# Two attention layers: stacks of queries and keys moved in rows of 2 KB, score units by heads of the keys, and the end of the first stage in another order

## The reference

```python
def layer0(x, y):                       # per batch: 128 channels x 1024
    q, k = conv(Wq0, bq0, y), conv(Wk0, bk0, y)         # 8 heads of 16 channels
    attn = softmax(q_heads @ k_heads.T / sqrt(128))
    o = conv(Wo0, bo0, attn @ conv(Wv0, bv0, x)) + x
    return (o - mean(o)) * rsqrt(var(o) + eps) * gn_w + gn_b
def layer1(h, y):                       # h, y: 32 x 128 x 1024
    q = (h @ Wq + 2 * (h @ Aq @ Bq)).heads(32)
    k = (y @ Wk + 2 * (y @ Ak @ Bk)).heads(8)           # each repeated for 4 heads of q
    v = (y @ Wv + 2 * (y @ Av @ Bv)).heads(8)
    ctx = softmax(q @ k.T / sqrt(32)) @ v
    return h + ctx @ Wo + 2 * (ctx @ Ao @ Bo)
```

## Time and profile before

| | |
|---|---|
| median of 3 runs | 1451.95 us (1450.32 to 1458.22) |
| the profiled execution: its own time | 1455.78 us |
| its span from first to last instruction | 1453.7 us |
| mean granted clock of TensorE | 0.975 |
| TensorE (PE) busy | 1361.1 us, 94% |
| VectorE, ScalarE, GpSimd busy | 917.0, 823.9, 194.5 us |
| moved by DMA | 342.34 MB in 374,128 packets, mean 235 GB/s |

### The profile page before, as it was taken

One profiled execution on the slowest core, in us unless ns is written; L12 is line 12 of the kernel. 1 busy time (PEld: TensorE's weight loads), 2 busy tenths in 40 slices (PEclk: granted clock), 3 DMA queues, 4 the chain that ended last, 5 costly groups with the idle time before them and its releaser, 6 DMA issues.

```text
span 1453.7 us, 23720 instructions
## 1 busy us (share of the span) xinstructions
PE 1361.1 (94%) x7135; PEld 1063.2 (73%) x7135; DVE 917.0 (63%) x2061; ACT 823.9 (57%) x2913; POOL 194.5 (13%) x157
## 2 busy tenths in 40 slices
PE   7999999999979999999999988879999999999998
PEld 5778887777768788888888876556666667666666
DVE  5666666656644577777776743446677757666665
ACT  4566666555631177777775735446666667666441
POOL 5433333555522000000000000000000000000000
PEclk8999999999989999999999999889999999999999
DMA  6465665887946889999998899999899999998982
GB/s 181 164 218 197 196 202 191 268 262 242 301 160 215 241 238 259 265 251 261 259 260 237 238 317 304 292 274 247 217 250 249 244 239 241 243 235 217 241 224 80
DMA packets 374128, 342.34 MB, mean 235 GB/s; under 512 B 24242, under 2 KB 304404, under 8 KB 373108
## 3 DMA queue, kind: packets, MB, share of 16 engines
q1 hardware_dynamic: 374004, 340.84, 85.2%
HBM read 224.37 MB, written 116.39 MB: 234 GB/s over the span
## 4 chain that ended last, share of the span: by engine, by line
PE 71%; DMA 13%; DVE 4%; ACT 4%; issue 3%; SPq 3%; POOL 2%; ACTq 0%; DVEq 0%; POOLq 0%
PE bank L640 21%; PE bank L677 15%; PE bank L536 10%; DMA q_stack<-lse_dram 9%; PE bank L695 6%; PE bank L724 4%; PE bank L735 4%; PE bank L486 2%; PE bank L611 2%; PE bank L596 1%; ACT lora_aT_kv L874 1%; PE bank L523 1%; SPq L1683 1%; DMA x_in<-in_x 1%; POOL o_split L1479 1%
## 5 line engine op out<-in xcount | busy, mean ns | idle before, releaser
L932 ACT ACTIVATE bank<-bank,negs 128x128 f32<-128x128 f32 x1024 | 349.1, 343 | 221.9 <-DVE negs L1188 221.6
L640 PE MATMUL bank<-hT,wq 128*128 128x512 f32 x1488 | 391.5, 403 | 0.0
L677 PE MATMUL bank<-wo,op 128*128 128x512 f32 x1344 | 353.6, 401 | 2.0 <-DVE h_blk L1265 2.0
L640 PEld LDWEIGHTS bank<-hT,wq 128*128 128x128 f32 x1488 | 267.1, 190 | 47.4
L1183 DVE TENSOR_REDUCE maxes<-bank 128x4 f32<-128x512 f32 x256 | 176.3, 689 | 189.9 <-PE bank L695 187.4
L677 PEld LDWEIGHTS bank<-wo,op 128*128 128x128 f32 x1344 | 251.2, 192 | 53.6 <-DVE op L1235 2.4
L949 ACT ACTIVATE probT<-bank 128x512 f32<-128x512 f32 x256 | 151.4, 604 | 149.8 <-PE bank L724 147.0
L932 ACT ACTIVATION_READ_ACCUMULATOR bank<-bank,negs 128x1 f32 x1024 | 211.8, 207 | 0.0
L536 PE MATMUL bank<-wkv_hi,yT 128*128 128x512 f32 x512 | 206.2, 424 | 0.0
L695 PEld LDWEIGHTS bank<-k_stack,q_stack 96*128 96x128 f32 x1024 | 152.2, 192 | 25.1 <-DMA q_stack<-q_dram 6.9
L695 PE MATMUL bank<-k_stack,q_stack 96*128 96x128 f32 x1024 | 147.3, 267 | 6.7 <-DMA q_stack<-q_dram 5.6
(11 more groups left out here) (167 smaller groups left out, 1668.3 us busy)
## 6 DMA issues: line engine op xcount, KB each, us to landing
q_dram<-q_part SPq DMA_DIRECT2D x192, 256.0 KB, 3.6
q_stack<-q_dram SPq DMA_DIRECT2D x256, 192.0 KB, 5.1
q_stack<-q_dram SPq DMA_DIRECT2D x64, 768.0 KB
k_stack<-k_dram SPq DMA_DIRECT2D x128, 192.0 KB, 4.6
y_in<-in_ctx SPq DMA_DIRECT2D x32, 512.0 KB, 4.4
x_in<-in_x SPq DMA_DIRECT2D x32, 512.0 KB, 5.2
h_dram<-h_out SPq DMA_DIRECT2D x32, 512.0 KB, 2.8
h_in<-h_dram SPq DMA_DIRECT2D x32, 512.0 KB, 6.1
```

The lines of the kernel that those rows point to most:

```text
L640: m = pe.matmul(bank(u % 2).rearrange("p (a n) -> p a n", a=2), wq[:, block, part, c, :], hT[(group + 1) % 2][:, :, of, c, :], start=c == ...
L677: mm = pe.matmul(out_bank(pair, m), op[m][:, of, c, :], wo[m][:, w, c, :], start=c == 0 and of == 0 and w == 0, stop=c == GROUP - 1 and of ...
L932: act.activation(part, part, ACT.Exp, bias=negs[:, n % RING, g:g + 1], scale=SCORE1, accum_out=sums[:, score_column(k), g, member:member + ...
```

## The change

- A unit of scores is now one head of keys with its four heads of queries, instead of one head of queries out of each of the four heads of keys. Its load is 96 rows of 2 KB that lie together in `q_dram`, instead of 96 rows of four pieces of 512 B. The matmuls are as many and as large as before. Units run through the first halves of four batches and then through the second halves (`score_half`).
- `k_dram` holds the keys as they are stacked, (3 x 32) x 4 x 128. A load of keys is 96 rows of 2 KB instead of 96 x 4 pieces of 512 B, both for the units and for the scores made again. The store of a batch's keys is six transfers of 128 pieces of 512 B, instead of two (256 pieces of 512 B and 256 of 1 KB).
- `q_part` holds two blocks of queries; three stores for two blocks, in pieces of 1 KB instead of 512 B.
- A raw piece of Wo is loaded in one transfer instead of four; mixed pieces are made one batch ahead, and the order of the pieces and their loads changes with it.
- Units start at slot 24 instead of 40, are taken in every slot up to 232, in every third up to 256, and then in five slots of 16 instead of eight. The second group of logarithms is taken at slot 224, in the middle stage.
- At the end of the first stage h of the third batch is loaded earlier, the turned h are rounded and split earlier, TensorE transposes before it projects, and the first projections wait for fewer of them.

```diff
-        k_dram = scratch("k_dram", (HALVES, P, 3, P))
+        k_dram = scratch("k_dram", (HALVES, 3 * HD, GQ, P))
...
-        for i in range(4 * GROUP + 1):
+        for i in range(4 * GROUP + 2):
             c, member = divmod(i, 4)
-            made = {0: [(0, c, 0, 0)], 1: [(3, c, 4, 4 * c + 1)], 2: [(5, c, 2, 0), (4, c, 1, 4 * c + 2)],
-                    3: [(1, c, 3, 0), (2, c, 4, 4 * c + 3)]}[member]
+            made = {0: [(2, c - 1, 4, 4 * c - 1), (0, c, 0, 0)], 1: [(6, c - 1, 4, 4 * c)],
+                    2: [(3, c, 4, 4 * c + 1), (5, c, 2, 0)], 3: [(4, c, 1, 4 * c + 2), (1, c, 3, 0)]}[member]
...
-        FIRST_SCORES, LAST_TURN = 40, QUERY_SLOTS - 4 * NC
+        FIRST_SCORES, LAST_TURN, LAST_EARLY = 24, QUERY_SLOTS - 4 * NC, QUERY_SLOTS - AHEAD - 5
...
-                if chunk == 0:
+                if w < QUERY_SLOTS:
                     log_slot[chunk] = w
-                    rest = w + 8
+                    rest = w + (4 if chunk else 8)
...
-            if w < LAST_TURN:
-                take = w % 16 != 15 and (n % GROUP or w < LAST_TURN - 5)
+            if w < LAST_EARLY:
+                take = True
             elif w < QUERY_SLOTS:
-                take = w % 2 == 0
+                take = w % 3 == 0
             else:
-                take = i in range(9 if pair in log_steps else 1, STEP, 2)
+                take = i % 3 == 1 and (i > 9 or pair not in log_steps)
...
+        def score_half(n):
+
+            group, of = divmod(n // GQ, GB * NQ)
+            q, b = divmod(of, GB)
+            return NQ * (GB * group + b) + q
...
-        FIRST_STACK_LAST = LAST_TURN - 8
+        FIRST_STACK_LAST = LAST_EARLY - 4
...
-                if quarter == 0:
-                    pe.wait_ge(S["hT_lo"], 4 * (both + 1))
+                if quarter < 2:
+                    pe.wait_ge(S["hT_lo"], 4 * both + 3 + quarter)
...
-                for g in range(GQ):
-                    m = pe.matmul(score_bank(n)[:, g * P:(g + 1) * P], q_stack[place // GROUP][SCORE_ROWS, g, member, :],
+                for j in range(GROUP):
+                    m = pe.matmul(score_bank(n)[:, j * P:(j + 1) * P], q_stack[place // GQ][SCORE_ROWS, g, j, :],
                                   k_stack[SCORE_ROWS, k % 2, g, :], start=True, stop=True)
...
-                    for g in range(GQ):
-                        sp.dma_start(w_raw[i][g * HD:(g + 1) * HD, :], rows[g, :, of]).then_inc(S[f"w_raw{i}"], DMA)
+                    sp.dma_start(w_raw[i][:], rows[:, :, of]).then_inc(S[f"w_raw{i}"], DMA)
...
-                keys = k_dram[NQ * b:NQ * (b + 1)].rearrange("q p a t -> p q a t")
-                sp.dma_start(keys[:, :, 0, :], f32(kT_sb[b % 2][:, :, 0, :])).then_inc(S[f"kv_out{b % 2}"], DMA)
-                sp.dma_start(keys[:, :, 1:3, :].rearrange("p q a t -> p q (a t)"),
-                             f32(kT_sb[b % 2][:]).rearrange("p q a t -> p q (a t)")).then_inc(S[f"kv_out{b % 2}"], DMA)
+                for q in range(NQ):
+                    rows = k_dram[NQ * b + q].rearrange("(d a) g t -> a g d t", a=3)
+                    for row, part in ((0, 0), (1, 0), (2, 1)):
+                        sp.dma_start(rows[row], f32(kT_sb[b % 2][:, q, part, :])).then_inc(S[f"kv_out{b % 2}"], DMA)
...
-                sp.dma_start(f32(q_stack[score_place[n] // GROUP][SCORE_ROWS, :, member, :]),
-                             q_dram[k, :, :, member * P:(member + 1) * P].rearrange("(g d) a n -> (d a) g n", g=GQ)).then_inc(
+                sp.dma_start(f32(q_stack[score_place[n] // GQ][SCORE_ROWS, g, :, :]).rearrange("r j n -> r (j n)"),
+                             q_dram[k, g * HD:(g + 1) * HD].rearrange("d a n -> (d a) n")).then_inc(
...
-                sp.dma_start(f32(k_stack[SCORE_ROWS, 2 + k % 2, :, :]),
-                             k_dram[k].rearrange("(g d) a t -> (d a) g t", g=GQ)).then_inc(S[f"again_in{k % 2}"], DMA)
+                sp.dma_start(f32(k_stack[SCORE_ROWS, 2 + k % 2, :, :]), k_dram[k]).then_inc(S[f"again_in{k % 2}"], DMA)
```

More of the change, by code:

```diff
@@ L190, in xattn_two_layers @@
         at[0] = q_place
+        s2_sb = sb("s2_sb", [P, BANK])
+        h_blk = [sb(f"h_blk{i}", [P, BANK]) for i in range(2)]
+        lse_rows = sb("lse_rows", [P, 1, 2, P])
+        at[0] = q_place + 4 * 2 * GB * 2 * P
         op[6] = sb("op6", [P, 2, GROUP, P], F32R)
@@ L248, in raw_in @@
                 return DMA * ((n - FIRST_Q) // 2 + 1)
-            return (DMA * NC if raw_of(n) < 2 else 0) + DMA * GQ * ((n - FIRST_O) // 4 + 1)
+            return (DMA * NC if raw_of(n) < 2 else 0) + DMA * ((n - FIRST_O) // 4 + 1)
         def raw_piece(n):
@@ L995, in scalar_program @@
                 softmax0(b)
+                if last:
+                    round_hT(0)
                 if b:
@@ L1223, in split_op @@
                 elif m == 1:
-                    dve.wait_ge(S["lse_out0"], DMA)
+                    dve.wait_ge(S["lse_out1"], DMA)
                 elif m == 6:
-                    for i in range(2):
-                        dve.wait_ge(S[f"q_out{i}"], 3 * DMA * NC * NG // 2)
+                    dve.wait_ge(S["q_out1"], 3 * DMA * NC * NG // 4)
                 elif m:
@@ L1245, in combine @@
                     if pair == 0:
-                        for i in range(2):
-                            dve.wait_ge(S[f"h_out{i}"], DMA * B // 2)
+                        dve.wait_ge(S["q_out0"], 3 * DMA * NC * NG // 4)
                     else:
@@ L1635, in put_q @@
                 for row, part in ((0, 0), (1, 1), (2, 0)):
-                    sp.dma_start(halves[:, row, :, :], f32(q_part[u % 2][:, part, :]).rearrange(
-                        "p (b n) -> p b n", b=GB)).then_inc(S[f"q_out{u % 2}"], DMA)
+                    sp.dma_start(halves[:, row, :, :], f32(q_part[pair % 2][:, part, :, :, :]).rearrange(
+                        "p b j n -> p b (j n)")).then_inc(S[f"q_out{pair % 2}"], DMA)
             def wait_queries(k):
                 last = queries_out(k)
-                for u in (last - 1, last):
-                    sp.wait_ge(S[f"q_out{u % 2}"], 3 * DMA * (u // 2 + 1))
@@ L1777, in sync_program @@
                     finish_unit(n)
-            for b in range(2, GB):
-                load_h(b)
+            load_h(3)
             write_kv(B - 1)
```

208 lines of the change are left out of this document (107 added, 101 removed).

## The result

The changed kernel takes 1495.99 us (median of 4 runs, 1491.85 to 1498.87), the kernel before 1452.95 in the runs beside it. That is a ratio of 1.029, 95% interval 1.025 to 1.033. It is 43 us slower, where the forecast was 6 us faster. The profiled execution has a span of 1495.2 us. From its page: the busy times of the engines, the granted clock and the DMA share in 40 slices of 37.4 us, and the packets.

A forecast was written before the change was run, and what follows sets the result against it. TensorE was taken as the bound in each part, leaving only its waiting to gain. Terms -27 + 0 + 2 - 9 + 28 = -6 us took 1452 to 1446 us; range 1418 to 1474, the forecast's own 1434 to 1458.

The forecast's parts named there:

- Keys and Wo on four engines, +28: First stage while Wo is prepared: transfers with outer count 4 run on four engines, making x late; +28 us, bounds 0 to +55.
- The sign to look for: While Wo is prepared: x_hi late in two batches of four, with waits for x_in and batches of 14 to 16 us.
- Larger rows, -27: Middle and last parts: 2 KB rows land stacks sooner, cutting TensorE's waits and the half clock behind them; -27 us, bounds 0 to -47.
- The small waits: TensorE's waits after 1010 us, thirteen of 0.95 us on average and one of 2.8 us: 11 us taken off.
- the wait near 870 us: TensorE's wait of 4.3 us for queries of a score unit should go, through the new order of loads.
- the long waits: Four waits from 880 to 1010 us, 21.9 us, behind 2 MB Wo loads: 1.3 us off each, 6 us with what adds up.
- Units moved, 0: 28 score units, 11.2 us, move from the last part to the middle, both bound by TensorE: sum 0.
- Late there, +2: Scores start at slot 24, six slots after their queries may be loaded; being late there adds 2 us, 0 to 6.
- The first stage's end, -9: Loading h of the third batch earlier and waiting for half of the turned h saves 9 us, 0 to -13.
- The signs: Middle part some 8 us longer than 478 us; last part 30 to 35 us shorter than 527.
- The first, free narrow transfers: Key and Wo transfers cost nothing, spread over all engines or hidden by slack: 1418 us, chance 0.22.
- The second and third: Second: narrow transfers cost more in batches 17 to 29, 1470 us, chance 0.24. Third: 2 KB rows don't help, 1464 us, 0.14.

The follow-up runs named there:

- both wide: Changed kernel, key stores and Wo loads given an outermost DRAM count of 128 instead of 4, keys and Wo rows permuted: 1454.75 us, ratio 1.001 to 1.005 to before.
- experiment 2: Kernel with both wide, stacks laid out in SBUF so each 2 KB row arrives as four pieces of 512 B: 1459.95 us, 1.005 to 1.010 to before.
- keys by column: Changed kernel, Wk and Wv columns ordered by column then head, a batch's keys in three stores, raw Wo pieces in four loads: 1461.11 us.
- Experiment 5: On the twelve-store kernel, 2 MB loads spread: 1482.81 against 1485.33 us. On keys by column, no units in slots 233 to 255: 1453.09; then seventh load later: 1451.88 us.
- experiment 4: Changed kernel with twelve key stores and four Wo loads, third batch's h load moved behind its batch's stores: 1488.60 us against 1485.33.
- experiment 1: Changed kernel, outer DRAM count 128 instead of 4: both 1454.75 us, keys alone 1468.36, Wo alone 1472.09. Kernel before, keys in six stores of count 4: 1486.08.

## Why the prediction was wrong, step by step

By its own terms, for the profiled executions: forecast -6, measured +41.5 (1495.2 against 1453.7). Two terms make up nearly all of the 47.5 us between: the relief of 27 us that did not come, and the charge of 28 us that was 20 too small.

- **Keys and Wo on four engines, +28.** Right in mechanism, and the engine count was right; the size was off. The last 14 batches took 48 us more than before: 39.5 by the narrow transfers (222.8 against 183.2 with both wide), and 8.3 that stay with both wide. The time per batch was nearly right: 61.4 us for four batches is 15.35 each, measured 15.9. I charged 12 batches instead of 14 (5 us) and took off 4 us for slack. The 0.55 us in each of 14 batches that are left (8 us) I put down to SyncE standing at its issues and to the clock (0.88 from 250 to 430 us, with both wide 0.96); no run tells the two apart. The rest, some 2 us, is that batches of before took 12.5 on average (174.9 / 14) and not 12.65. The sign to look for was wrong as well: it shows as the wait of the copy for the store of the keys, 29.5 us, and only 7.1 us for x. I had checked when x would land, and not when the buffer of the keys would be free. Before Wo is prepared a batch stayed at 11.75 us, as worked out.
- **Larger rows, -27.** This step failed. With both transfers wide, middle and last stage together are 0.1 us longer than before (+22.8 - 22.7); the rows themselves are worth some 4 us (experiment 2). It had three parts. The small waits went, though not by larger rows, and in their place TensorE waits for exponentials of ScalarE (two of its groups in the last stage, the last column its idle time: the kernel before, 926:1453, then the kernel with both wide, 947:1452).

```profile
L724 PE MATMUL bank<-q_stack,k_stack 98*128 98x512 f32 x238 | 103.6, 437 | 31.2 <-DMA q_stack<-lse_dram 29.7 <-ACT probT L949 1.1
L735 PE MATMUL bank<-probT,v_in 128*32 128x512 f32 x480 | 66.7, 628 | 0.6 <-DVE lse_rows L1211 0.4
```
```profile
L731 PE MATMUL bank<-q_stack,k_stack 98*128 98x512 f32 x238 | 101.0, 426 | 19.4 <-DMA q_stack<-lse_dram 18.8 <-ACT probT L958 0.6
L742 PE MATMUL bank<-probT,v_in 128*32 128x512 f32 x480 | 65.7, 619 | 12.9 <-ACT probT L958 12.8
```

  29.7 us of waits for lse_dram become 18.8, and 12.8 us before the contexts are new. It may be that fewer units stand between a product of scores and its context, five in 16 slots instead of eight; this is not shown, and six instead of five did not shorten the wait (13.2 us from 880 to 1445 us, against 12.2 with five, both with keys by column). The second part, the wait near 870 us, went, but the next load of keys then stood behind two loads of 2 MB, and TensorE waited 9.4 us for it. The piece of SyncE's order that I cited ended at those two loads; its next row was this load. Third, the long waits did not get 6 us shorter: from 880 to 1050 us TensorE waited 24.7 us for DMA before, and waits 34.3 us with the rows of 2 KB. Experiment 5 speaks for engines that are full there, at a share near 1, and against the order of the queue.
- **Units moved, 0.** Half right: 28 units add 11.2 us to the middle, which has 15.8 us more of busy TensorE. The remaining 4.6 us go with a granted clock of 0.98 instead of 0.99, and idle time grew from 15.7 to 22.8 us. "Late there, +2" did not occur: TensorE has no wait for queries of a unit from slot 24 on.
- **The first stage's end, -9.** Right: from the last x_hi to the projections it is 44.2 us before and 35.9 with both wide, -8.3 (39.2 in the changed kernel, -5.0). But in the kernel with both wide the last 14 batches take 8.3 us more than before, 5.1 of them in the last one (17.2 us instead of 12.1), so the stage comes out even. The number of stores of keys is not it (three of them: 184.1 us against 183.2), nor, by experiment 4, the load of h. In that last batch ScalarE stands until a piece of Wo is stored, which the kernel before does not do there:

```profile
399.53 0.62 ACT L856 CAST o_split<-w_mix 128x512 fp32r<-128x512 f32 x1 [5.07 <-DMA wo_dram<-o_split]
```

  That points at the new order of the pieces, which no run changed alone: the cause stays open.
- **The signs.** A last part 30 to 35 us shorter: 23.8. A middle 8 us longer: 23.4. The sum had made the two nearly cancel in my favour, and they do cancel.
- **The rivals.** The first, free narrow transfers, is refuted by experiment 1. The second and third both happened, 1470 and 1464 us each; I gave them apart and added nothing for both together, which is 24 + 18 = 42 us above 1446, 1488, near the result. Both were worked out from rows, and neither excludes the other; the range should have held their sum. That 1488 comes near 1496 is in part luck: the first part of it was sized by eight late episodes of x, which are not what the trace shows.

The 512 B for line rate of the Trainium skill ("DMA: Bandwidth & Descriptors", table "Specifications"), from which the prediction drew that larger rows would gain no bandwidth, is not borne out by the share of the engines (0.97 to 0.84 for the same bytes). That next to no time was gained has another reason: from 550 to 850 us TensorE was not waiting.

## What to carry to other kernels

A layout that makes loads contiguous moves its cost to the stores: look at the outermost count of both sides of every transfer that changes, count its engines by small packets or by the DMA share while it runs alone, and count its issues, since here SyncE's time was as scarce as the engines'. Price a relief only where the waiting engine waits, and ask of a wait that goes which load is next in the queue. When two rivals are independent, work out the time when both come true.

## What the runs showed of the hardware

- SyncE does not only queue its issues; with transfers piled up they take longer. Six stores of keys took 8.68 us at 352 us in the changed kernel, 3.4 us before Wo was prepared, and 2.9 us in most batches of the kernel with both wide. Three stores of queries took 8.50 us at 926 us, behind loads of 2 MB that use all 16 engines, and 2.0 us near 600 us. What the limit is no run here shows.
- While SyncE stood at narrow transfers and issued nothing else, the share was 0.27 for 7 us, at 99 GB/s; four of 16 engines are 0.25.
- A stride in SBUF, of 16 bytes on the write or of 128 bytes on the read, took ScalarE's rounding of 128 x 512 from 0.62 to 1.12 to 1.15 us. From PSUM, read with a stride of 128 bytes and written in a row, the copy of the same size stayed at 0.59 us.
